# Second attention of a two-layer kernel: the first score of each pair waits for both banks

## The reference, cut to what matters

```
q = (x @ wq).reshape(B, T, 32, 16)
k, v = x @ wk, x @ wv                     # one set for all heads
scores = einsum('bqhd,bkd->bhqk', q, k) / sqrt(16)
scores = where(tril(ones(T, T)), scores, -inf)
out = einsum('bhqk,bkd->bqhd', softmax(scores), v)
return out.reshape(B, T, 512) @ wo
```

## Time and profile before

| | |
|---|---|
| median of 3 runs | 2202.95 us (2199.75 to 2222.36) |
| the profiled execution | 2218.44 us, span 2216.7 us |
| busy in the span | TensorE 2008.4 us, VectorE 1167.0, ScalarE 883.8, GpSimd 480.9 |
| mean granted clock of TensorE | 0.933 |
| second attention | 1546.4 to 2070 us of the span, 16 steps |
| scores (line 1642) | 640 matmuls, 213.9 us busy, mean 459 ns |
| exponentials (line 1549) | 640, 309.6 us busy, mean 563 ns |

### The profile page before, as it was taken

The page is one execution under the profiler, slowest core; times in us unless marked ns, Lnnn a source line. Parts: engine busy times, 40 slices in busy tenths (PEclk is TensorE's granted clock), DMA queues, the critical chain, the costliest instruction groups (busy, mean ns, idle before and its releaser), DMA issues. The chain is left out here.

```text
span 2216.7 us, 34036 instructions
## 1 busy us (share of the span) xinstructions
PE 2008.4 (91%) x12632; PEld 1153.7 (52%) x12632; DVE 1167.0 (53%) x2541; ACT 883.8 (40%) x1861; POOL 480.9 (22%) x376
## 2 busy tenths in 40 slices
PE   5858999999999999999976899996999999999698
PEld 4535666656666656665643454553444444444244
DVE  3536555565555555556401454445676676673166
ACT  3402444444444444444430122221566665665222
POOL 0011444444443434444330000000000000000000
PEclk8867999999999999999997999995899999998699
DMA  9742232222333233322208221126132122211201
GB/s 310 254 136 58 58 78 57 58 60 70 78 78 78 68 78 78 78 55 55 67 23 258 67 67 52 51 93 138 21 51 46 34 49 47 37 30 22 92 29 48
DMA packets 100856, 172.19 MB, mean 78 GB/s; under 512 B 25738, under 2 KB 46378, under 8 KB 100562
## 3 DMA queue, kind: packets, MB, share of 16 engines
q1 hardware_dynamic: 100690, 170.01, 29.2%
HBM read 84.32 MB, written 29.38 MB: 51 GB/s over the span
## 5 line engine op out<-in xcount | busy, mean ns | idle before, releaser
L822 ACT ACTIVATE at_prob<-at_scp 128x512 f32<-128x512 f32 (+1 forms) x608 | 349.6, 575 | 533.1 <-PE at_scp L923 524.5
L856 DVE CUSTOM_DVE_ANT_0 at_junk<-at_mxp,causal 128x128 f32<-128x128 f32 (+3 forms) x512 | 240.5, 486 | 339.6 <-PE at_mxp L932 334.9
L1549 ACT ACTIVATE as_prob<-as_scp 128x512 f32<-128x512 f32 (+2 forms) x640 | 309.6, 563 | 202.2 <-PE as_scp L1645 149.5
L932 PE MATMUL at_mxp<-l_khi,at_qhi 96*128 96x512 f32 (+2 forms) x768 | 262.4, 406 | 24.9 <-DMA at_qhi<-at_shi 21.1
L919 PE MATMUL at_scp<-at_qhi,l_khi 97*128 97x512 f32 (+1 forms) x608 | 260.4, 428 | 8.2 <-issue 4.5
L1599 DVE TENSOR_REDUCE as_mxd<-as_mxp 128x2 f32<-128x256 f32 (+3 forms) x256 | 203.6, 821 | 105.3 <-PE as_mxp L1664 103.4
L922 PE MATMUL at_scp<-at_qlo,l_khi 96*128 96x512 f32 (+1 forms) x608 | 235.0, 387 | 0.0
L923 PE MATMUL at_scp<-at_qhi,l_klo 96*128 96x512 f32 (+1 forms) x608 | 233.6, 384 | 0.0
L1584 POOL TENSOR_TENSOR l_att_t<-l_att_t,as_spread 64x1024 f32<-64x1024 f32 x16 | 37.9, 2368 | 878.9 <-DMA as_spread<-l_recips 878.9
L1642 PE MATMUL as_scp<-as_q,l_keys 49*128 49x512 f32 (+2 forms) x640 | 213.9, 459 | 13.4 <-ACT as_prob L1549 10.8
L1659 PE MATMUL as_mxp<-l_keys,as_q 48*128 48x512 f32 (+2 forms) x768 | 186.9, 467 | 35.7 <-DVE as_mxf L1597 13.9
(11 more groups left out here) (204 smaller groups left out, 2742.1 us busy)
## 6 DMA issues: line engine op xcount, KB each, us to landing
at_qhi<-at_shi SPq DMA_DIRECT2D x192, 128.0 KB, 2.4
at_qlo<-at_slo SPq DMA_DIRECT2D x192, 128.0 KB, 2.4
op_ring<-in_wmod SPq DMA_DIRECT2D x12, 1024.0 KB, 6.2
op_ring<-in_wo_t SPq DMA_DIRECT2D x8, 1024.0 KB, 13.6
at_spread<-l_recips SPq DMA_DIRECT2D x64, 128.0 KB, 2.8
l_o<-at_u_sb SPq DMA_DIRECT2D x16, 512.0 KB, 3.2
ml_o_t<-l_o SPq DMA_DIRECT2D x16, 512.0 KB, 4.2
as_q<-scratch_queries SPq DMA_DIRECT2D x48, 128.0 KB, 4.7
```

What stands on the lines that cost most here:

```text
L822: nc.scalar.activation(prob[:, x % RING0, c0:HALF], scp[x % BANKS0][:, c0:HALF], ACT.Exp).then_inc(s["exp_done"], 1)
L856: nc.vector.tensor_tensor_reduce(out=junk[:, u % 2, 0:w], in0=tile[:, 0:w], in1=k.causal[:, HALF - w:HALF], scale=1.0, scalar=LOWEST, op0= ...
L932: nc.tensor.matmul(bank("max", t, u)[:, 0:w], qhi[t % 2][0:KR, j, qt * P:(qt + 1) * P], k.khi[0:KR, t // NG, k0:k0 + w], start=True, stop= ...
L1549: nc.scalar.activation(prob[:, x % RING1, cols], scp[x % BANKS1][:, cols], ACT.Exp).then_inc(s["exp_done"], 1)
```

## The change

The first score of a pair (`jj == 0`) waits for one exponential more than before, so that its own bank and the bank of its partner are free. The second score has no wait. With x the number of the first score, the count was x - 2 for the first and x - 1 for the second; it is now x - 1 for the first alone. All matmuls, their order, and the banks stay as they are.

```
                     diagonal = kt >= 4 * qc
-                    if x >= BANKS1:
-                        pe.wait_ge(s["exp_done"], x + 1 - BANKS1)
+                    if jj == 0 and x + 2 > BANKS1:
+                        pe.wait_ge(s["exp_done"], x + 2 - BANKS1)
                     mm = nc.tensor.matmul(out, k.keys[rows, t // NG, kt * P:(kt + 1) * P], queries, start=True, stop=not diagonal)
```

## The result

The changed kernel is slower by 3%: ratio 1.0295 (95% interval 1.0256 to 1.0334), median 2273.0 us (2265.0 to 2292.7, four runs) against 2209.5 (2199.8 to 2222.4, four runs; the 2203 of the forecast was the median of the first three). Forecast were 33 us more, 1.5%, 2236 us, in a range to 2262; measured are 63.5 us more. The sign is right; the time lies outside the range. Over the four executions of the changed kernel the time follows TensorE's mean granted clock: 2292.7 us at 0.902, 2276.8 at 0.911, 2269.2 and 2265.0 at 0.920. The profiled execution is the slowest of the four, 2292.7 us, 74.2 above that of before; the second attention takes 81 us more in it, the rest of the kernel 7 less.

What follows compares the result with a forecast made beforehand. The second attention was taken to go at TensorE's pace, set by when each matmul group starts. 2203 us plus 30.2 for ScalarE's delay and 3 for clock falls gave 2236 us, 1.5% slower; range 2213 to 2262 us.

Steps and rivals of the forecast that it cites:

- The chain through ScalarE: Second attention's bursts: first scores' longer wait delays ScalarE's exponentials and pair D; 1.89 us a step, 30.2 us in all.
- That nothing takes it back: Second attention: waits for VectorE before the maxima do not absorb the delay of 1.89 us a step.
- That removing the second wait saves nothing: Second scores of pairs: dropping 319 waits gains nothing, since each follows a score waiting for the same count.
- the clock: Middle steps of the second attention: two more stretches at 1.2 GHz than now, adding 3 us; bounds 8 gained, 30 lost.
- The first two and last two steps: Steps 0, 1, 14 (lower clock, less loss) and 15 (ScalarE-bound, more loss) were left against each other.
- The rival of more falls: Second attention: two or more low-clock stretches a step add 16 us and up, giving 2250 to 2270 us; chance 0.12.
- The rival of pairing: Split score pairs starting together free TensorE array time, up to 42 us saved, giving 2161 us; chance 0.06.

Runs made afterwards that it cites:

- the second wait's run: Changed kernel with the second score's wait kept, for the same count as the first score's; ratio to the kernel before 1.0253 (1.0218 to 1.0289).

## Why the prediction was wrong

- *The chain through ScalarE* was right, with its places. At the full clock D is behind A by 3.63 us in quads 4 and 5 (forecast 3.64), 3.85 in quads 0 and 1 (by the working 1619.66, 3.87 behind A at 1615.79), 3.85 in quads 6 and 7 (3.87) and 3.95 in quads 8 and 9 (3.94), and the step is 33.5 us, shown by the second wait's run. The sum of 1.89 us a step was measured as 1.9.
- *That nothing takes it back* was right at the full clock, since the whole 1.9 us arrive in the step. Its argument was weaker than it looks. The 16.5 us of waits for VectorE were those of the maxima's matmuls alone; their weight loads waited for it 35.0 + 10.8 = 45.8 us more. In the same way the 52.5 us before line 1642 were 10.8 of the matmuls and 41.8 of the weight loads. *That removing the second wait saves nothing* is borne out by the second wait's run within its interval.
- *The term that failed is the clock:* "I take two more than now, 3 us, nearest to the present rate." The two stretches below are steps 2 to 13 before and after:

```profile
1615.80:2003.70 387.90, 365.74 (x3568) 186.25 (x3564) 266.72 (x312) 243.15 (x516) 28.66 (x13) 0.98 0.25 41
1617.50:2067.80 450.30, 396.06 (x3566) 182.40 (x3564) 269.26 (x312) 252.07 (x516) 29.34 (x13) 0.83 0.21 36
```

In the profiled executions they take 62.4 us more. Of these the chain is 12 x 1.9 = 22.8; about 40 are the clock, whose mean there went from 0.98 to 0.83. Median against median, 63.5 us less 30 for the chain leaves 33 for the clock: the term was set at a tenth of what it measured. Even the upper bound, 30 us for two falls of 3.4 us in each step, was too low, because a fall can last 10.2 us: I took the length of a fall as fixed. The price of a microsecond at the lower clock was not too low (1.6 us for 3.4 before, 4.0 for 13.6 in the second wait's run); its amount was, 149 us in place of 17. The rate now was the wrong row to lean on. The prediction itself said that the stretches without values grow by 0.3 to 0.7 us; the run with one burst changed shows that 0.54 us is enough for a fall in every step. And the kernel before already had long falls, outside the steps from which the term was taken. This is one in its step 1; one in step 14 is as long, and one in step 15 lasts 16.6 us:

```profile
1593.80:1604.00 10.20, 10.20 (x64) 4.89 (x58) 6.22 (x7) 6.28 (x13) 0.00 (x0) 0.50 0.01 2
```

- *The first two and last two steps* were set off against each other. Both ends cost more than the chain. The last two take 77.1 us instead of 65.9 (2067.8 and 2003.7 to the last score), 11 us for twice 1.9, at clocks of 0.69 and 0.77; the first two take 77.2 us instead of 69.4, at 0.76 and 0.83. How the 11 us divide between ScalarE's round, which no maxima cover there, and the clock no run shows.
- *The rival of more falls* had the right mechanism, with a chance of 0.12 and a price of 16 us and up; its 2250 to 2270 us end just below the 2273 measured.
- *The rival of pairing* is refuted: where it would have shortened the step by 2.6 us, the step at the full clock grew by 1.9, and 12 more matmuls in it cost the changed kernel 0.1 us (33.6 against 33.5). TensorE's own work isn't far away, though: the same 12 cost the kernel before 1.4 us (33.0 against 31.6).

What stays open: why a fall lasts 3.4 us in one place and 10.2 in another, and so how many a given schedule will have, and why the order with values after every quad comes to the same 31.6 us at the full clock.

## What to carry to other kernels

A wait that is moved to the earlier instruction of a pair can cost nothing on its own engine and still take the head start of the engine behind it. Write down the round (end of use, semaphore, producer, semaphore, use) and compare it with the consumer's rate, here 1.25 us against 0.97; it costs most where several rounds follow one another (1.9 us a step against 0.3). Before pricing idle time on TensorE, look whether the granted clock already falls anywhere in this stage, and how long the longest fall is: then idle time can cost three times its length (0.54 us cost 1.5 to 1.7), and the range has to hold long falls in every step.

## What the runs showed of the hardware

Adding work to TensorE made a kernel faster. One matmul of 384 columns over 128 partitions in each idle spell of 0.3 to 0.5 us kept the granted clock of steps 2 to 13 at 1.00 where it was 0.83, and took the changed kernel from 1.030 to 1.011. The Trainium skill, page "TensorE: Matmul & The Clock Gate", section "A second HAM failure mode: psum-queue depth-cycling", tells of short idle times between groups of matmuls, in a loop over PSUM banks, that make the clock go back and forth; the trace agrees, with idle spells of at most 0.51 us before the pairs of the bursts shown and 13.6 of 37.5 us at the lower clock.
